# First attention of a two-layer kernel: the maxima's key rows in a transfer of their own, and a wait for two transfers where there was one for five

## What is computed

```python
q_c = (c_q @ Wq_up).reshape(b, s, N_HEADS, HEAD_DIM)     # 4 wide
q_r = (x @ Wq_rope).reshape(b, s, N_HEADS, ROPE)         # 64 wide
scores = (einsum('bqhd,bkhd->bhqk', q_c, k_c) + einsum('bqhd,bkd->bhqk', q_r, k_r)) / scale
attn = softmax(scores, axis=-1)
out = einsum('bhqk,bkhd->bqhd', attn, v_c).reshape(b, s, N_HEADS * HEAD_DIM) @ Wo
```

## Time and profile before

| | |
|---|---|
| median of 3 runs | 2617.37 us (2616.24 to 2623.03) |
| the profiled execution, as a run | 2618.33 us |
| its span, first to last instruction | 2616.4 us |
| TensorE matmuls busy | 2486.5 us, 95% |
| TensorE weight loads busy | 1839.7 us, 70% |
| VectorE / ScalarE / GpSimd busy | 60% / 52% / 40% |
| the first attention's steps | from about 51 to 1400 us of the span |

### The profile page before, as it was taken

The page is one execution under the profiler, slowest core; times in us unless marked ns, Lnnn a source line. Parts: engine busy times, 40 slices in busy tenths (PEclk is TensorE's granted clock), DMA queues, the critical chain, the costliest instruction groups (busy, mean ns, idle before and its releaser), DMA issues. The chain is left out here.

```text
span 2616.4 us, 40097 instructions
## 1 busy us (share of the span) xinstructions
PE 2486.5 (95%) x12487; PEld 1839.7 (70%) x12487; DVE 1558.7 (60%) x2791; ACT 1355.7 (52%) x2088; POOL 1059.2 (40%) x1097
## 2 busy tenths in 40 slices
PE   6999999999999999999998599989999999999996
PEld 3677776777777777777774366667887878778774
DVE  5666666666666666666663611066657557557566
ACT  3577777777777777777774300033324324334231
POOL 0455565555556555555653100034234234343220
PEclk8999999999999999999998699989999999999998
DMA  5222222222222222221221500021010010010001
GB/s 190 48 47 55 43 54 49 46 51 51 51 43 54 47 48 51 45 57 43 54 44 57 160 6 0 0 81 41 0 40 16 24 40 16 24 40 16 1 1 53
DMA packets 46694, 116.86 MB, mean 45 GB/s; under 512 B 5313, under 2 KB 22721, under 8 KB 40514
## 3 DMA queue, kind: packets, MB, share of 16 engines
q1 hardware_dynamic: 46658, 116.40, 17.0%
HBM read 71.81 MB, written 10.49 MB: 31 GB/s over the span
## 5 line engine op out<-in xcount | busy, mean ns | idle before, releaser
L472 DVE TENSOR_REDUCE row_max<-ps_max 128x1 f32<-128x512 f32 x1024 | 671.0, 688 | 198.5 <-PE ps_max L539 176.6
L390 POOL TENSOR_TENSOR p_lo<-probs,p_hi 128x1024 f16<-128x1024 f32 x256 | 547.8, 2150 | 387.4 <-ACT p_hi L422 387.1
L417 ACT ACTIVATE probs<-ps_score 128x1024 f32<-128x1024 f32 x512 | 523.2, 1022 | 253.3 <-PE ps_score L554 229.1
L552 PE MATMUL ps_score<-Q,K 128*128 128x512 f32 x1024 | 407.5, 398 | 1.6 <-ACT probs L417 1.5
L554 PE MATMUL ps_score<-Q,K 97*128 97x512 f32 x1024 | 407.0, 397 | 0.0
L539 PE MATMUL ps_max<-KX,Q 68*128 68x512 f32 x1024 | 378.6, 410 | 16.1 <-DMA KX<-content_k 10.3
L466 DVE TENSOR_TENSOR Q<-ps_x,Q 64x512 fp32r<-64x512 f32 x256 | 176.5, 689 | 247.2 <-ACT Q L412 243.5
L422 ACT ACTIVATE p_hi<-probs 128x1024 f16<-128x1024 f32 x256 | 269.5, 1053 | 4.1
L539 PEld LDWEIGHTS ps_max<-KX,Q 68*128 68x128 f32 x1024 | 188.7, 189 | 91.7 <-issue 40.2
L552 PEld LDWEIGHTS ps_score<-Q,K 128*128 128x128 f32 x1024 | 194.4, 190 | 60.9 <-ACT probs L417 13.4
L554 PEld LDWEIGHTS ps_score<-Q,K 97*128 97x128 f32 x1024 | 195.2, 191 | 38.8
(11 more groups left out here) (231 smaller groups left out, 4223.7 us busy)
## 6 DMA issues: line engine op xcount, KB each, us to landing
Q<-Q SPq DMA_DIRECT2D x64, 512.0 KB, 4.3
w_raw<-in_w_qrope SPq DMA_DIRECT2D x32, 512.0 KB, 3.7
wq_raw<-in_wq SPq DMA_DIRECT2D x8, 1024.0 KB, 5.5
wo_raw<-in_wo SPq DMA_DIRECT2D x8, 1024.0 KB, 4.9
w_raw<-in_w SPq DMA_DIRECT2D x6, 704.0 KB, 4.2
Q<-content_q SPq DMA_DIRECT2D x64, 64.0 KB
K<-content_k SPq DMA_DIRECT2D x64, 64.0 KB
wkv_raw<-in_wkv SPq DMA_DIRECT2D x8, 512.0 KB, 3.5
```

Source lines behind the costliest of these rows:

```text
L390: pool.tensor_tensor(p_lo[:, j, :, :], probs[:, j, 0:PAIRED, :], p_hi[:, j, :, :], ALU.subtract)\
L417: act.activation(probs[:, j, 2 * half:2 * half + 2, :], ps_score[half][:, :, :], ACT.Exp, scale=SCALE).then_inc(exped, 1)
L472: dve.tensor_reduce(row_max[:, t, j:j + 1], ps_max[t % 2][:, :], axis=AXX, op=ALU.max)\
L552: pe.matmul(ps_score[half][:, k, :], K1[:, b, t * P:(t + 1) * P], Q1[:, b, j, :], start=True, stop=False)
```

## The change

The transfer of `KX` is taken out of `content` and becomes `max_keys`, with the semaphore `max_in`, which the first transfer of `content` (4 rows of `Q2`) now raises too. For step n+2 `max_keys` is issued right behind the row of step n, when the last maxima of that step have been taken. `m00` waits for `max_in` (32 per group); the wait for the other three transfers (`content_in`, now 48 per group) stands at `s00`. Before the loop `max_keys` goes ahead of `content` for both batches.

```diff
--- before.py
+++ after.py
@@ -252,6 +252,7 @@
         q_high = sem("q_high")
         q_low = sem("q_low")
         q_copied = [sem(f"q_copied{b}") for b in range(NB)]
+        max_in = [sem(f"max_in{b}") for b in range(NB)]
         content_in = [sem(f"content_in{b}") for b in range(NB)]
         max_made = sem("max_made")
         max_taken = sem("max_taken")
@@ -308,22 +309,29 @@
                 sp.dma_start(w_raw[:, :, :, :].rearrange("p c a n -> p c (a n)"),
                              w_view[:, :, bass.ds(g * 2 * P, 2 * P)]).then_inc(w_in, 16)
 
+            def rows(tile, src, g, b, row, parts, landed):
+                at = ROPE + row * HD0
+                sp.dma_start(tile[at:at + parts * HD0, b, :, :].bitcast(F32),
+                             dram[src][bass.ds(g * GH, GH), 0:parts * HD0, b * S:(b + 1) * S].rearrange("h r t -> r h t"))\
+                  .then_inc(landed, 16)
+
+            def max_keys(g, b):
+                rows(KX, "content_k", g, b, 0, 1, max_in[b])
+
             def content(g, b):
-
-                for tile, src, row, parts in ((Q2, "content_q", 0, 1), (Q2, "content_q", 1, 2),
-                                              (K2, "content_k", 0, 2), (K2, "content_k", 2, 1),
-                                              (KX, "content_k", 0, 1)):
-                    rows = dram[src][bass.ds(g * GH, GH), 0:parts * HD0, b * S:(b + 1) * S].rearrange("h r t -> r h t")
-                    at = ROPE + row * HD0
-                    sp.dma_start(tile[at:at + parts * HD0, b, :, :].bitcast(F32), rows).then_inc(content_in[b], 16)
+                rows(Q2, "content_q", g, b, 0, 1, max_in[b])
+                rows(Q2, "content_q", g, b, 1, 2, content_in[b])
+                rows(K2, "content_k", g, b, 0, 2, content_in[b])
+                rows(K2, "content_k", g, b, 2, 1, content_in[b])
 
             def copy_q(n, b):
                 sp.wait_ge(q_high, 2 * n + 2)
                 sp.dma_start(Q1[0:ROPE, b, :, :].bitcast(F32), Q2[0:ROPE, b, :, :].bitcast(F32)).then_inc(q_copied[b], 16)
 
             load_w(0)
-            content(0, 0)
-            content(0, 1)
+            for b in range(NB):
+                max_keys(0, b)
+                content(0, b)
             copy_q(0, 0)
 
             def body(g, first, last):
@@ -331,6 +339,8 @@
                     n = 2 * g + b
                     sp.wait_ge(row_made, n + 1)
                     sp.dma_start(Q2[MROW:MROW + 1, b, :, :].bitcast(F32), mrow[0:GH, :].bitcast(F32)).then_inc(row_in, 16)
+                    if not last:
+                        max_keys(g + 1, b)
                     if b == 0 and not last:
                         sp.wait_ge(w_split, 2 * g + 2)
                         sp.sem_inc(gate_sp, 1)
@@ -531,7 +541,7 @@
                 if j % 2 == 0 and t == 0:
                     pe.wait_ge(q_high, 2 * n + j // 2 + 1)
                 if j == 0 and t == 0:
-                    pe.wait_ge(content_in[b], 80 * (g + 1))
+                    pe.wait_ge(max_in[b], 32 * (g + 1))
                     if wait_free:
                         pe.wait_ge(row_made, n)
                 if wait_free:
@@ -545,6 +555,7 @@
                     pe.wait_ge(q_low, 2 * n + 2)
                     pe.wait_ge(q_copied[b], 16 * (g + 1))
                     pe.wait_ge(row_in, 16 * (n + 1))
+                    pe.wait_ge(content_in[b], 48 * (g + 1))
                 if wait_free:
                     pe.wait_ge(exped, 8 * n + 2 * j + half - 1)
                 for k in range(2):
```

## The result

The changed kernel takes **2604.48 us** (median of 6 runs, 2604.26 to 2609.6) against 2617.53 for the kernel before in its 6 runs (2613.13 to 2623.03). The ratio is 0.9952, 95% interval 0.9938 to 0.9966: 13 us, 0.48% faster, more than the 0.3% that can be told from no change. The forecast was 2605.5.

The account below looks back on a forecast made before the run. TensorE's matmuls, busy 95% of 2616.4 us, bound the kernel; only standing still could be won. 13.6 - 1.4 - 0.4 = 11.8 us off 2618.33 gave 2606.5, or 2605.5 with the runs' median 1.0 lower; range 2602.5 to 2617.

Parts of the forecast that it names:

- The size of the wait: TensorE's weight loads before the maxima: 39.6 us in 62 gaps, less 26.0 us of ordinary change, leaves 13.6 us waiting for content.
- Term 1: At the maxima: needing only KX, issued a step early, and the first Q transfer, they gain the whole 13.6 us.
- Term 2: At the first score: the row's landing decides next; it comes 0.6 us sooner, so a step can win up to 0.7 us.
- Term 3: Waiting steps in the loop: six with waits over 0.7 us keep the rest, 1.4 us together.
- Term 4: TensorE, ahead of each first score: one more semaphore wait, hidden behind two maxima; 0.4 us taken for a few steps.
- Terms 5 and 6: SyncE's moved issues cost nothing; w_raw comes up to 0.3 plus about 0.4 us later, hidden by GpSimd's waits for p_hi.
- A: At the first score: the row, held by slow content reads, replaces KX as the wait; about 2614 us, chance 0.27.
- B: At the first score: KX issued right behind the row delays it; 0.3 us net gives +12 us, 2629; chance 0.06.
- C: At the maxima: the first Q transfer is itself late, so the edit takes no effect; 2617 us, chance 0.03.

## Why the prediction was right

**The size of the wait** (first part): 13.6 us was read off as 39.6 less 62 floors of 0.42 us. The load's gaps fell to 26.3 us, by 13.3, and the time from the first row to the last by 12.4. That the floor was taken from undisturbed steps, and not the matmul view's 10.3 us taken for the whole, was worth 3 us.

**Term 1** held in size, the whole gain at the maxima. Its reason was put too narrowly: it named KX and the first Q transfer as what the maxima would have to wait for. With all five in the wait the gain is the same.

**Term 2** carried the sum, and it held. The row was said to come 0.6 us sooner, between 0 and 1.0: it comes 0.75 sooner after its own issue, 0.65 sooner after the first content issue. The most that the row needs by itself was put at 2.27 us; it is 1.92. The whole win of 0.7 us per step that followed from it was enough nearly everywhere. The figure from the Trainium skill, "DMA: Bandwidth & Descriptors", Specifications (an engine's bandwidth, an estimated 0.28 us for KX), is below what the runs show for a share, 0.65 us taken out and 1.4 us put in; by it the sum would have been 9 us.

**Term 3** is the term that was mis-sized. Six steps were to keep 1.4 us. The first score's load is indeed late by over 0.1 us in six steps, 1.4 us together. This is the difference between the line of the change (2.4 us in 8, two of them as before) and that of the kernel before, less the load's ordinary 0.04 us in each of the six:

```profile
PEld ps_score L552 <- issue: 0.7, 2, 0.4
```

But a late load is not yet a late matmul. In the worst step

```profile
124.20 0.30 PEld L549 LDWEIGHTS ps_max<-KX,Q 68*128 68x128 f32 x2 [0.42 <-issue]
124.20 0.73 PE L549 MATMUL ps_max<-KX,Q 68*128 68x512 f32 x2
...
124.87 0.19 PEld L563 LDWEIGHTS ps_score<-Q,K 128*128 128x128 f32 x1 [0.37 <-issue]
124.87 0.49 PE L563 MATMUL ps_score<-Q,K 128*128 128x512 f32 x1
...
125.21 0.39 PE L565 MATMUL ps_score<-Q,K 97*128 97x512 f32 x1
```

the first score's matmul starts 0.67 us behind the maxima's instead of 0.57, the only one that is late by over 0.1 us, and the next one follows after 0.34 us instead of 0.24. Over all 62 steps the first scores lose 0.2 us and the matmuls behind them 0.4: 0.6 us where the term took off 1.4.

That six steps are late again is partly luck. The term took the six long waits of one execution to be six steps that keep their rest. Only one of them, at 124 us, is late with the change; in the other five the row now lands 1.5 to 2.2 us sooner, and five steps whose load had waited 0.13 us at most are late instead. Over the 62 steps the row's landing times of the two executions have nothing in common (correlation -0.08), and between the kernel before and the run that splits the wait alone, with the same order of transfers, it is -0.12. So which steps are slow changes from execution to execution; what the forecast could use is how many there are.

**Term 4**, 0.4 us for the added wait, is nothing: two more cost nothing measurable. Both terms took off 1.8 us, the runs show 0.6. 13.3 less 0.6 is 12.7 us, and 12.4 went between the first row and the last, against a forecast of 11.8. That the spans differ by 13.9 and not by 12.4 is chance, behind the loop.

**Terms 5 and 6** held. The two waits of GpSimd before, from 80 to 1400 us:

```profile
POOL p_lo L390 <- ACT p_hi L422: 384.9, 168, 6.9
POOL w_hi L355 <- DMA w_raw<-in_w_qrope: 214.5, 31, 78.8
```

and, with SyncE's waits beside the earlier trace rows, after:

```profile
POOL p_lo L400 <- ACT p_hi L432: 356.2, 152, 6.3
POOL w_hi L365 <- DMA w_raw<-in_w_qrope: 231.5, 31, 79.4
...
SPq L329 <- ACT Q L422: 476.0, 63, 8.7
SPq L352 <- PE ps_score L565: 464.4, 62, 7.6
```

w_hi waits 17.0 us more for w_raw in 31 steps, 0.55 us each, within the 0.7 put down. The waits for p_hi behind it shrank by 28.7 us: they took up the delay, and the rest is about what the steps became shorter by. TensorE's loads show no longer wait for p_lo (0.5 us once in either kernel). SyncE still waits 7.6 us a step before the copy and 7.5 before the content.

**The rivals.** A did not come about in the change, but it is real: with KX second or fourth the row does take over the wait. B has its proof against it in the 64 KB behind the row; the danger that it named is on the other side, KX ahead of the row. C: with the change the first Q transfer's last update comes 2.73 us after its issue, over 3 us early.

The rule cited for A, from the Trainium skill, "DMA: Bandwidth & Descriptors", Queues, rings and completion order (an engine's increment lands after every earlier write of that engine), agrees with what the updates show: the row's last one follows the content's last one by 0.19 us before (5.98 and 5.79) and by 0.18 after (5.32 and 5.14). It did not lead to rival A's 2614 us, since the content's last update comes 0.65 us sooner without KX. By itself, as in the last step before, the row needs 1.92 us.

## What to carry to other kernels

A small transfer that someone waits for pays for what is queued ahead of it: from its issue to its landing the row took 1.92 us with nothing ahead, 2.24 with four transfers, 2.99 with five and 4.38 with six. For what was queued behind it it paid nothing (2.23 with 96 KB behind). If a buffer comes free early, load it early and behind the urgent transfer, not in one block with what comes free last. To size a wait, take the gaps of the weight loads and subtract the gap of undisturbed steps, and where the load runs ahead of its matmul, as at the first score, subtract that room too: with KX fourth, gaps of 21.8 us were 7.4 us of late matmuls and 4.3 us behind them. Then ask what stands right behind the removed wait in the same queue: with the row landing 0.9 us later than with the change (6.22 against 5.32 us) nothing was left of the 13 us. Do not carry the slow steps of one execution over to the next by name. And try the order of a block before you settle on it: 32 KB moved from the last to the second place of five cost 50 us, against the run that splits the wait and keeps the order.

## What was not expected

- The order of five transfers with the same bytes changes the landing of the last by 0.9 us (5.98 against 6.90 us after the first issue), and the kernel by 50 us. It hangs neither on KX's HBM addresses nor on the partitions it is written to. The packets of one stretch take three times as long; the mechanism stays open.
- A share of 32 KB has no fixed price in such a chain: 0.65 us taken out, 1.4 us put in.
- A first score that stops costs more than its idle time: in the step above with KX second, the next matmul starts 0.33 us after it (730.38 against 730.05), where in a running chain it is 0.23 to 0.24. So a stop costs a further 0.1 us: 3.2 us in the run with KX ahead of the row, 5.5 with KX second.
- Runs with long stops in the steps also lost some of TensorE's clock. With KX second the granted clock stood at 0.50 for 13.7 us between the first row and the last, with one more share for 30.7 us; before and with the change never. Each time a stop of 1.6 us or more lay just ahead of it, but most stops of that length were not followed by a lower clock.
